# An LSTM recurrence on one core: all four gates in one 32-row block, instead of two pairs side by side

## What is computed

```python
xW = einsum('ntd,dg->ntg', x, Wx) + b
def step((h, c), xw_t):
    a = xw_t + h @ Wh                  # (2, 1024): i, f, o, g, 256 each
    i, f, o = sigmoid(a[:, 0:256]), sigmoid(a[:, 256:512]), sigmoid(a[:, 512:768])
    g = tanh(a[:, 768:])
    c = f * c + i * g
    h = o * tanh(c)
x = x + hs
ys = cond / sqrt(256)
d = rsqrt(einsum('bi,io->bo', ys * ys, w * w) + 1e-8)
x = x + einsum('bsi,io->bso', x * ys[:, None, :], w) * d[:, None, :]
```

## Time and profile before

| | |
|---|---|
| median of 3 runs | 2189.81 us |
| the profiled execution, its own time | 2191.25 us |
| its span in the trace | 2189.1 us |
| TensorE clock granted, mean | 0.999 |
| busy: TensorE matmul / weight loads | 1620.9 us (74%) / 1334.2 us (61%) |
| busy: DVE / ACT / POOL | 1265.5 us (58%) / 851.6 us (39%) / 216.4 us (10%) |
| steps | 1024, 2.09 us each inside a loop body |

### The profile page before, as it was taken

The page is one execution under the profiler, slowest core; times in us unless marked ns, Lnnn a source line. Parts: engine busy times, 40 slices in busy tenths (PEclk is TensorE's granted clock), DMA queues, the critical chain, the costliest instruction groups (busy, mean ns, idle before and its releaser), DMA issues.

```text
span 2189.1 us, 201141 instructions
## 1 busy us (share of the span) xinstructions
PE 1620.9 (74%) x88232; PEld 1334.2 (61%) x88232; DVE 1265.5 (58%) x12316; ACT 851.6 (39%) x4100; POOL 216.4 (10%) x1289
## 2 busy tenths in 40 slices
PE   5777777777777777777777777777777777777777
PEld 4666666666666666666666666666666666666664
DVE  3555555555555555555555555555555555555554
ACT  2433333333333333343333333333433333333332
POOL 0010101010110101010101101010101011010100
PEclk9999999999999999999999999999999999999999
DMA  2000000000000000000000000000000000000001
GB/s 84 0 0 0 0 0 0 0 0 0 0 0 0 0 0 0 0 0 0 0 0 0 0 0 0 0 0 0 0 0 0 0 0 0 0 0 0 0 0 38
DMA packets 4427, 6.67 MB, mean 3 GB/s; under 512 B 1090, under 2 KB 2882, under 8 KB 4420
## 3 DMA queue, kind: packets, MB, share of 16 engines
q1 hardware_dynamic: 3872, 5.51, 0.7%
q10 hardware_dynamic: 548, 1.05, 0.1%
HBM read 4.46 MB, written 2.10 MB: 3 GB/s over the span
## 4 chain that ended last, share of the span: by engine, by line
PE 54%; DVE 29%; ACT 10%; issue 6%; DMA 0%; SPq 0%; POOLq 0%; POOL 0%
PE pA L192 53%; DVE turned L294 12%; DVE junk L298 11%; ACT gates L157 10%; DVE hst L306 5%; DVE gates L298 1%; PE pO L246 1%; DMA w_sb<-in_w_dram 0%; PE pD L167 0%; SPq L101 0%; PE pA L181 0%; PE pD L199 0%; DVE ores L314 0%; DVE wsq L274 0%; PE pA L174 0%
## 5 line engine op out<-in xcount | busy, mean ns | idle before, releaser
L192 PE MATMUL pA<-wh_sb,hst 128*2 128x64 f32 (+1 forms) x65536 | 1105.8, 219 | 545.3 <-DVE hst L306 544.3
L192 PEld LDWEIGHTS pA<-wh_sb,hst 128*2 128x2 f32 (+1 forms) x65536 | 922.0, 90 | 821.6 <-DVE hst L306 818.3
L157 ACT ACTIVATE gates<-turned 128x8 f32<-128x8 f32 x2048 | 442.9, 216 | 1167.8 <-DVE turned L294 1045.9
L294 DVE STREAM_TRANSPOSE turned<-pA 128x64 f32<-128x64 f32 x2048 | 512.0, 250 | 641.8 <-PE pA L192 554.4
L298 DVE CUSTOM_DVE_ANT_0 junk<-gates 128x4 f32<-128x4 f32 x4096 | 506.8, 161 | 80.0
L162 ACT ACTIVATE tanhc<-gates 128x2 f32<-128x2 f32 x2048 | 418.7, 204 | 132.2
L306 DVE TENSOR_TENSOR hst<-tanhc,gates 128x4 f32<-128x4 f32 x2048 | 337.1, 165 | 172.5 <-ACT tanhc L162 162.0
L181 PE MATMUL pA<-wx_sb,xr 128*8 128x64 f32 (+1 forms) x16448 | 419.2, 219 | 1.3 <-issue 1.3
L167 PE MATMUL pD<-wh_sb,picks 128*32 128x128 f32 x2096 | 397.9, 274 | 0.0
L298 DVE DVE_READ_ACCUMULATOR2_ANT gates<- 128x1 f32 x4096 | 337.3, 83 | 0.0
L181 PEld LDWEIGHTS pA<-wx_sb,xr 128*8 128x8 f32 (+1 forms) x16448 | 293.6, 94 | 1.6 <-issue 1.6
(11 more groups left out here) (26 smaller groups left out, 9.0 us busy)
## 6 DMA issues: line engine op xcount, KB each, us to landing
outT_dram<-ores SPq DMA_DIRECT2D x8, 256.0 KB, 2.5
xh<-in_xT_dram SPq DMA_DIRECT2D x6, 320.0 KB, 7.9
wx_sb<-in_Wx_dram SPq DMA_DIRECT2D x1, 1024.0 KB, 5.2
wh_sb<-in_Wh_dram ACTq DMA_DIRECT2D x1, 1024.0 KB, 7.6
w_sb<-in_w_dram SPq DMA_DIRECT2D x1, 256.0 KB, 8.4
xh<-in_xT_dram SPq DMA_DIRECT2D x2, 64.0 KB, 7.6
bias_sb<-in_bT_dram ACTq DMA_DIRECT2D x2, 2.0 KB
condT<-in_condT_dram ACTq DMA_DIRECT2D x1, 2.0 KB, 5.4
```

The costliest lines, as they stand in the source:

```text
L157: act.activation(gates[:, j, :, 0:3 * G].rearrange("p b (a q c) -> p a q b c", a=PAIR, q=PAIR)[:, :, :, :, 0], turned[:, j, :].rearrange(" ...
L192: last = pe.matmul(into(st, j, c, M), hst[:, st, k, lo:lo + M], chunk(wh_sb[:, k, :], c, j, pair), start=False, stop=True, skip_group_chec ...
L294: dve.transpose(turned[:, j, :], pA[st][j][:, 0:PAIR * Q]).then_inc(turned_ready[j], 1)
```

## The change

`T` is 2 instead of 4, so the loop body has 4 steps and runs 256 times. Each gate has its own rows: gate g is in rows 4g to 4g+3 of a quadrant, and all gates share the same 32 columns. A matmul moves 32 columns instead of 64. Rows are reached by windows of 2(t+1) + 4g columns, and h is written in four copies. The transposes read 32 columns instead of 64. The sigmoid reads the same number of values per partition as before. Per step there are now 64 matmuls with h (before 32), 32 with x (before 8), 4 with the bias on average (before 2), and one filler. The bias comes by four transfers of one row, instead of two.

```diff
-    T = 4
+    T = 2
     ROWS = T * B
     SETS = 2
     BODY = SETS * T
     NBODY = SEQ // BODY
-    PAIR = G // 2
-    AT_B = ROWS
-    SLOT = 4 * ROWS
+    WINDOW = G * ROWS
+    SLOT = G * WINDOW
...
-        def chunk(of, c, j, pair):
-            return of.rearrange("p (g d) -> p g d", d=D)[:, PAIR * pair:PAIR * pair + PAIR, j * P + c * Q:j * P + (c + 1) * Q]
+        def chunk(of, c, j, g):
+            return of[:, g * D + j * P + c * Q:g * D + j * P + (c + 1) * Q]
...
-            return hst[:, blk % SETS, j, at:at + 6 * ROWS].rearrange("p (a r) -> p a r", a=2)[:, :, 0:B]
+            return hst[:, blk % SETS, j, at:at + G * (WINDOW + ROWS)].rearrange("p (g r) -> p g r", g=G)[:, :, 0:B]
...
-                        act.activation(gates[:, j, :, 0:3 * G].rearrange("p b (a q c) -> p a q b c", a=PAIR, q=PAIR)[:, :, :, :, 0],
-                                       turned[:, j, :].rearrange("p (q a r) -> p a q r", q=PAIR, r=ROWS)[:, 0:PAIR, :, B * t:B * (t + 1)],
+                        act.activation(gates[:, j, :, 0:3 * G:3].rearrange("p b g -> p g b"),
+                                       turned[:, j, 0:WINDOW].rearrange("p (g r) -> p g r", g=G)[:, :, B * t:B * (t + 1)],
                                        ACT.Sigmoid).then_inc(gates_ready[j], 1)
...
-                return pA[st][j][c * Q:c * Q + rows, 0:PAIR * Q].rearrange("p (g u) -> p g u", u=Q)
+                return pA[st][j][c * Q:c * Q + rows, 0:Q]
...
-            def fill_x(st, j, k, pair):
-                lo, hi = (0, AT_B + ROWS) if pair else (AT_B, AT_B + ROWS)
+            def fill_x(st, j, k, g):
+                M = ROWS * (g + 1)
                 for c in range(G):
-                    last = pe.matmul(into(st, j, c, hi - lo), xr[:, st, k, lo:hi], chunk(wx_sb[:, k, :], c, j, pair),
+                    last = pe.matmul(into(st, j, c, M), xr[:, st, k, WINDOW - M:WINDOW], chunk(wx_sb[:, k, :], c, j, g),
                                      start=False, stop=False, skip_group_check=True)
...
-            def rec(st, t, j, k, pair):
-                lo = SLOT * t + 2 * ROWS * pair
-                M = B * (t + 1) + AT_B * pair
-                for c in range(G):
-                    last = pe.matmul(into(st, j, c, M), hst[:, st, k, lo:lo + M], chunk(wh_sb[:, k, :], c, j, pair),
-                                     start=False, stop=True, skip_group_check=True)
+            def rec(st, t, j, k, lo=0, hi=G):
+                for g in range(lo, hi):
+                    at = SLOT * t + WINDOW * g
+                    M = B * (t + 1) + ROWS * g
+                    for c in range(G):
+                        last = pe.matmul(into(st, j, c, M), hst[:, st, k, at:at + M], chunk(wh_sb[:, k, :], c, j, g),
+                                         start=False, stop=True, skip_group_check=True)
                 return last
...
-                    rec(st, t, 0, 0, 0)
-                    rec(st, t, 0, 0, 1)
-                    rec(st, t, 1, 0, 0)
+                    rec(st, t, 0, 0)
+                    rec(st, t, 1, 0, 0, G // 2)
 
                     pe.wait_ge(h_ready[1], it * BODY + (s + 1))
-                    rec(st, t, 0, 1, 0)
-                    rec(st, t, 0, 1, 1).then_inc(sums_ready[0], 1)
-                    rec(st, t, 1, 0, 1)
-                    rec(st, t, 1, 1, 0)
-                    rec(st, t, 1, 1, 1).then_inc(sums_ready[1], 1)
+                    rec(st, t, 0, 1).then_inc(sums_ready[0], 1)
+                    rec(st, t, 1, 0, G // 2, G)
+                    rec(st, t, 1, 1).then_inc(sums_ready[1], 1)
...
-                        dve.transpose(turned[:, j, :], pA[st][j][:, 0:PAIR * Q]).then_inc(turned_ready[j], 1)
+                        dve.transpose(turned[:, j, :], pA[st][j][:, 0:Q]).then_inc(turned_ready[j], 1)
...
-                        dve.tensor_tensor(hcopies((s + 1) % BODY, j), tanhc[:, j, :].unsqueeze(1).broadcast_to([P, 2, B]),
-                                          gates[:, j, :, 6].unsqueeze(1).broadcast_to([P, 2, B]), ALU.mult).then_inc(h_ready[j], 1)
+                        dve.tensor_tensor(hcopies((s + 1) % BODY, j), tanhc[:, j, :].unsqueeze(1).broadcast_to([P, G, B]),
+                                          gates[:, j, :, 6].unsqueeze(1).broadcast_to([P, G, B]), ALU.mult).then_inc(h_ready[j], 1)
```

More of the change, by code:

```diff
@@ L40, in build @@
         wh_sb = sb("wh_sb", [P, K, G * D])
-        bias_sb = sb("bias_sb", [P, PAIR * D])
+        bias_sb = sb("bias_sb", [P, D])
         picks = sb("picks", [P, Q])
         xh = sb("xh", [P, K, B, SEQ + BODY])
-        xr = sb("xr", [P, SETS, K, AT_B + ROWS])
-        hst = sb("hst", [P, SETS, K, T * (SLOT + B) + 3 * ROWS])
-        turned = sb("turned", [P, K, PAIR * Q])
+        xr = sb("xr", [P, SETS, K, WINDOW])
+        hst = sb("hst", [P, SETS, K, T * (SLOT + B) + WINDOW])
+        turned = sb("turned", [P, K, Q])
         gates = sb("gates", [P, K, B, CELL])
@@ L117, in spread @@
             def spread(st, t):
-                pool.tensor_copy(xr[:, st, :, AT_B:AT_B + ROWS].rearrange("p k (t b) -> p k b t", b=B),
+                pool.tensor_copy(xr[:, st, :, WINDOW - ROWS:WINDOW].rearrange("p k (t b) -> p k b t", b=B),
                                  xh[:, :, :, t]).then_inc(xr_ready, 1)
@@ L143, in _ @@
             act.wait_ge(bias_zeroed, 1)
-            for pair in range(PAIR):
-                act.dma_start(bias_sb[pair * Q:pair * Q + 1, :], bT[:, pair * PAIR * D:(pair + 1) * PAIR * D]).then_inc(bias_loaded, 16)
+            for g in range(G):
+                act.dma_start(bias_sb[g * Q:g * Q + 1, :], bT[:, g * D:(g + 1) * D]).then_inc(bias_loaded, 16)
             act.wait_ge(demod_added, 1)
@@ L176, in fill_bias @@
                 return last
-            def fill_x(st, j, k, pair):
-                lo, hi = (0, AT_B + ROWS) if pair else (AT_B, AT_B + ROWS)
+            def fill_x(st, j, k, g):
+                M = ROWS * (g + 1)
                 for c in range(G):
-                    last = pe.matmul(into(st, j, c, hi - lo), xr[:, st, k, lo:hi], chunk(wx_sb[:, k, :], c, j, pair),
+                    last = pe.matmul(into(st, j, c, M), xr[:, st, k, WINDOW - M:WINDOW], chunk(wx_sb[:, k, :], c, j, g),
                                      start=False, stop=False, skip_group_check=True)
                 return last
-            FILLS = [(j, k, pair) for j in range(K) for k in range(K) for pair in range(PAIR)]
+            FILLS = [(j, k, g) for j in range(K) for k in range(K) for g in range(G)]
             SHARE = len(FILLS) // T
-            def rec(st, t, j, k, pair):
-                lo = SLOT * t + 2 * ROWS * pair
-                M = B * (t + 1) + AT_B * pair
-                for c in range(G):
-                    last = pe.matmul(into(st, j, c, M), hst[:, st, k, lo:lo + M], chunk(wh_sb[:, k, :], c, j, pair),
-                                     start=False, stop=True, skip_group_check=True)
+            def rec(st, t, j, k, lo=0, hi=G):
[5 more added lines that the diff above has]
+                                         start=False, stop=True, skip_group_check=True)
                 return last
@@ L201, in _ @@
             last.then_inc(demod_summed, 1)
-            pe.wait_ge(operands_ready, PAIR + 3)
+            pe.wait_ge(operands_ready, G + 3)
             for j in range(K):
@@ L206, in _ @@
             pe.wait_ge(xr_ready, 1)
-            for j, k, pair in FILLS:
-                last = fill_x(0, j, k, pair)
+            for j, k, g in FILLS:
+                last = fill_x(0, j, k, g)
             last.then_inc(filled, 1)
@@ L233, in _ @@
                         pe.wait_ge(xr_ready, it * SETS + (st + 2))
-                    for j, k, pair in FILLS[t * SHARE:(t + 1) * SHARE]:
-                        last = fill_x(1 - st, j, k, pair)
+                    for j, k, g in FILLS[t * SHARE:(t + 1) * SHARE]:
+                        last = fill_x(1 - st, j, k, g)
                     if t == T - 1:
@@ L253, in _ @@
             dve.wait_ge(picks_zeroed, 1)
-            for pair in range(PAIR):
-                dve.memset(picks[pair * Q:pair * Q + 1, AT_B * pair:AT_B * pair + ROWS], 1.0).then_inc(operands_ready, 1)
+            for g in range(G):
+                dve.memset(picks[g * Q:g * Q + 1, ROWS * g:ROWS * (g + 1)], 1.0).then_inc(operands_ready, 1)
             dve.memset(gates[:, :, :, :], 0.0).then_inc(buffers_zeroed, 1)
@@ L266, in _ @@
             g_cols = slice(G_ * D, (G_ + 1) * D)
-            dve.wait_ge(bias_loaded, 16 * PAIR)
-            dve.tensor_scalar(bias_sb[Q:Q + 1, D:PAIR * D], bias_sb[Q:Q + 1, D:PAIR * D], 2.0, None, ALU.mult).then_inc(operands_ready, 1)
+            dve.wait_ge(bias_loaded, 16 * G)
+            dve.tensor_scalar(bias_sb[G_ * Q:G_ * Q + 1, :], bias_sb[G_ * Q:G_ * Q + 1, :], 2.0, None, ALU.mult).then_inc(operands_ready, 1)
             dve.wait_ge(wx_loaded, 16)
@@ L285, in _ @@
             for j in range(K):
```

(2 more changed lines are left out.)

## The result

The changed kernel takes **4874.2 us** (median of 4 runs, 4780.14 to 4958.82) against 2189.18 for the kernel before on the same chip: ratio 2.194, 95% interval [2.181, 2.206]. The ratio compares fast runs alone, which of these four are the two of 4780.14 and 4826.42 us. The profiled execution took 4780.14 us, its span is 4778.3.

What follows compares the result with a forecast made beforehand. The prediction took a ring of engines waiting for each other, 2.09 us per step, as the bound; (34 - 36 + 5) ns x 1024 = +3 us and +2.5 us for loop ends gave 2196 us, range 2120 to 2330.

Steps and rivals of the forecast that it cites:

- the code no longer stays near the engine: Rival: the loop body's instructions are fetched again at each pass, 256 x 2.3 = 590 us, 2785 us in all; chance 0.02.
- Recurrent matmuls, +34 ns: Term for TensorE's matmuls with h: twice as many with half the columns cost 34 ns more per step.
- The distance of 29.2 ns: Time between groups of four recurrent matmul rows on TensorE, claimed to fall from 55.8 ns with 32 columns.
- issuing is fast enough when the queue is full: Step: 4 matmuls and 8 weight loads begin within 0.03 us, so TensorE can be fed a group in 29.2 ns.
- issue binds: Rival: a group's four matmuls need 8 ns each to issue, 32 ns a group, +89 us, 2285 us; chance 0.15.
- Transpose, -36 ns: Term for DVE's transpose of half 1: 32 fewer columns save 36 ns of its 250 ns per step.
- Write of h, +5: Term for writing h: 8 elements instead of 4 at 1.15 ns each add 5 ns per step.
- The rest of the ring: Links of the repeating chain of waits, 2.09 us per step, besides TensorE's recurrent matmuls: transpose, sigmoid, cell, write of h.
- Work with x and bias, 0 while covered: Term: TensorE's x and bias matmuls grow from 10 to 36 per step but cost nothing, fitting in idle time.
- Loop ends, +2.5 us, and POOL: Term: 128 more loop ends at up to 0.02 us add 2.5 us in all; waits on POOL stay met.
- The floor under short matmuls at 55.8 ns: Rival: the distance between groups of recurrent matmuls stays 55.8 ns at 32 columns, 3070 us; chance 0.10.
- A granted clock that stays at 1.00: Assumption for TensorE: the granted clock is 1.00, the level of 2.4 GHz, in the recurrent matmuls.

Runs made afterwards that it cites:

- b_pad8_pre56: The kernel before with 8 unused matmuls added behind each filler and 56 fillers before the loop instead of 24: 3052.5 us, ratio 1.397.
- a_pre0: The complete changed kernel without the 24 filler matmuls that stand before the loop: 2333.0 us, ratio to before 1.065.
- a_halfx: The changed kernel without the product of x with the k = 1 half of Wx, 340 matmuls in the body instead of 404: 2330.9 us, ratio to before 1.064.
- b_t2: The kernel before with T = 2 instead of 4 alone, 64-column matmuls kept: 2186.3 us, ratio to before 0.9987.

## Why the prediction was wrong

**The step that failed** is the last rival, "the code no longer stays near the engine". I named the cause, gave it 0.02 and 2785 us, and it came at 4874. Two errors are in it.

*Whether.* I held 1616 instructions against 2048 and stopped. What had to be held against it was the loop's place: blocks of 256, and a loop from 466 to 2090 touches eight of them. The same number of instructions 96 places earlier or 128 later touches seven, and stays. What stands before the loop can be counted in the kernel, and I didn't count it; the change raised its matmuls from 68 to 100, 272 to 400 instructions.

*How much.* I took 2.3 us per pass from the first body of the kernel before and scaled it by nothing. A fetched pass takes 30.6 us, about 3.4 us for each of its 9 fetched blocks in the mean, nearly whatever its work is (b_pad8_pre56: 30.7 us). A block holds 64 matmuls. Before, these were 1.5 steps, 3.1 us of work, which hid most of a block's time; in the change they are 0.6 steps, 1.4 us. A surcharge read where the cover was long was carried to where it is short. And the first body doesn't have the wait behind the branch back, 5.0 us in the mean of the 107 passes, which is the largest of the eight.

The sum, from the runs: 107 refetched passes x (30.56 - 8.90) = 2318 us; 148 others x (9.74 - 8.90) = 124 us, in which the clock is still low after the wait (0.88 in the window above; 0.996 is the mean of a_pre0); the layout itself 2333 - 2190 = 143 us. Together 2585, and the profiled execution is 2589 us over that of before.

**The forecast's own terms,** judged by a_pre0, where the code is out of the way:

- Recurrent matmuls, +34 ns: wrong, +0.19 us by the chain. The distance of 29.2 ns is right only for the first eight groups; the mean is 33.8. The step that failed here is "issuing is fast enough when the queue is full". That row shows a full queue, and I took a burst of 12 for a lasting rate. The rival "issue binds" (32 ns, 2285 us) fits what was measured and is near in size: a_pre0 is 2333. The term is short by some 160 ns. 144 of them are the 31 distances: 8 of 29.0 ns, the one of 53, two of 47 and 49 near the end of the step, and 20 of 33.4, together 1049 where I had 905. The other 16 are the last four rows, which start over 36 ns instead of 20. What causes the three long distances stays open.
- Transpose, -36 ns: measured 250 to 217, -33. Write of h, +5: 165 to 166, +1. The rest of the ring shrank by about 50 ns, where I had 31.
- Work with x and bias, 0 while covered: right. a_halfx (half of the x work) and a_pre0 (all of it) differ by 2 us.
- Loop ends, +2.5 us, and POOL: right that they hardly matter, but the sign is wrong; b_t2, with both and without the 32-column layout, is 2.7 us below before.
- The floor under short matmuls at 55.8 ns: refuted, 28 to 29 ns while the stock lasts. The rule of the Trainium skill's page "TensorEngine Tiling (Array Packing)", section "Instruction Overhead", taken by columns, gave 52 ns a group; the measurement decides against that reading. Its advice, not to tile a dimension that is small already, is right in this case for another reason, the lasting pace of 16.7 ns a matmul.
- A granted clock that stays at 1.00, which the sum took for granted: wrong, as a consequence of the waits and not a cause. It is 0.996 to 0.998 in the profiled executions of all resident variants of the short matmuls.

The forecast of 2196 would have been off even without the code: 2333 lies at the upper end of the range, just outside it.

## What to carry to other kernels

Before the number of instructions in a loop or ahead of it goes up, lay the loop out in the blocks in which the engine gets its code, and look at the instruction queue's row in the profile: it should show one fetch of the program and not megabytes. If it does show them, move the loop by some 100 instructions before anything else; here 32 idle matmuls in front were worth a factor of two. And read a rate of issue over a long stretch, not from the first rows after a wait: halving the columns of matmuls that start every 28 ns only helps if the engine can start them at twice the rate, and here its lasting pace was one float32 matmul every 16.7 ns.

## What was unexpected of the hardware

- A loop of 1616 to 1632 matmul and load instructions ran from one fetch when it touched seven blocks of 256, and was fetched again in 107 of 256 passes, or in 63 of 128, when it touched eight (both times from the same place, instruction 466).
- A fetched pass took 30.6 us for 404 matmuls and 30.7 us for 408, most of them twice as wide: about 3.4 us per fetched block of 64 float32 matmuls. The first wait in such a pass, behind the branch, was about 5 us.
- The lasting pace was one float32 matmul (two matmul and two load rows) every 16.7 ns, after some 16 matmuls at 12.7 ns (16 columns) or 14.5 ns (32 columns).
